# Building the table of routed rows with one-hot products instead of scattering it through memory

## The reference, cut to what matters

```
aff = sigmoid(x @ wa)                     # 16 experts per row
topk_p, topk_i = top_k(aff, 2)            # two experts per row
topk_p = topk_p / sum(topk_p)
combine = sum(one_hot(topk_i) * topk_p)   # [row, expert]
routed = einsum('bsed,bse->bsd', experts(x), combine)
shared = sum(shared_experts(x))           # two experts that every row uses
out = x1 + layernorm(x + shared + routed)
```

## Time and profile before

| what | us |
|---|---|
| median of 3 timed runs | 1720.22 |
| lowest and highest of them | 1716.72 and 1720.52 |
| span of the profiled execution | 1788.0 |
| scatters of the table issued from, to | 996.6, 1077.5 |
| readback of the table issued | 1171.3 |
| first product of the routed part | 1225.9 |

### The profile page before, as it was taken

The page is one execution under the profiler, slowest core; times in us unless marked ns, Lnnn a source line. Parts: engine busy times, 40 slices in busy tenths (PEclk is TensorE's granted clock), DMA queues, the critical chain, the costliest instruction groups (busy, mean ns, idle before and its releaser), DMA issues. The chain is left out here.

```text
span 1788.0 us, 22229 instructions
## 1 busy us (share of the span) xinstructions
PE 1513.8 (85%) x6687; PEld 950.7 (53%) x6687; DVE 835.7 (47%) x1747; ACT 767.9 (43%) x2028; POOL 535.1 (30%) x725
## 2 busy tenths in 40 slices
PE   4698989899889989986979736999999999999930
PEld 3454656565655656544768625886454444445510
DVE  4665676767668676655353401222222222222218
ACT  2677676777668687674231101111122112212205
POOL 2122322323222323222210570001433344444426
PEclk8787989899898989777999957999999999999975
DMA  5433554745554545535253502344577666565548
GB/s 162 81 58 65 106 131 96 148 90 143 98 120 113 117 101 102 131 86 205 106 187 133 95 13 82 106 92 128 127 217 188 177 146 175 143 141 123 91 60 362
DMA packets 115884, 225.61 MB, mean 126 GB/s; under 512 B 26661, under 2 KB 52854, under 8 KB 111160
## 3 DMA queue, kind: packets, MB, share of 16 engines
q1 hardware_dynamic: 96024, 182.70, 39.1%
q0 software_dynamic: 19744, 41.50, 12.4%
HBM read 219.28 MB, written 71.97 MB: 163 GB/s over the span
## 5 line engine op out<-in xcount | busy, mean ns | idle before, releaser
L2068 PE MATMUL bank<-ring,xg 128*128 x632 | 287.0, 597 | 1.0 <-issue 0.5
L1155 ACT ACTIVATE bank<-bank,mr 128x384 f32<-128x384 f32 (+3 forms) x512 | 255.5, 503 | 36.3 <-DVE mr L1380 36.3
L1380 DVE TENSOR_REDUCE mr<-bank 128x1 f32<-128x512 f32 (+3 forms) x352 | 214.8, 631 | 112.4 <-PE bank L1936 110.5
L1172 ACT ACTIVATE P<-bank 128x512 f32<-128x512 f32 x320 | 183.0, 596 | 109.2 <-PE bank L1950 107.5
L1833 POOL DMA_INDIRECT z_scratch<-wst,pl x79 | 125.0, 1582 | 281.0 <-DMA z_scratch<-wst,pl 249.8
L1934 PE MATMUL bank<-Ks,Qs 96*128 96x384 f32 (+3 forms) x512 | 173.3, 408 | 40.5 <-ACT P L1172 15.7
L1865 PE MATMUL bank<-xt,ws 128*128 128x512 f32 x768 | 186.7, 400 | 3.2 <-issue 3.2
L1690 DVE TENSOR_SCALAR wst<-bank,pl 128x512 f32<-128x512 f32 x79 | 59.3, 751 | 259.4 <-DMA z_scratch<-wst,pl 238.5
L2068 PEld LDWEIGHTS bank<-ring,xg 128*128 128x128 f32 x632 | 114.5, 191 | 118.0 <-issue 117.8
L1950 PE MATMUL bank<-Qs,Ks 98*128 98x512 f32 x320 | 154.8, 521 | 26.3 <-ACT bank L1155 12.1
L1764 POOL TENSOR_SCALAR_AFFINE_SELECT P<-P 128x256 f32<-128x256 f32 (+1 forms) x192 | 93.4, 488 | 279.3 <-ACT P L1172 276.9
(11 more groups left out here) (228 smaller groups left out, 2292.3 us busy)
## 6 DMA issues: line engine op xcount, KB each, us to landing
ring<-in_w SPq DMA_DIRECT2D x79, 1024.0 KB
ring<-in_w SPq DMA_DIRECT2D x79, 512.0 KB
Qs<-st SPq DMA_DIRECT2D x192, 128.0 KB, 4.9
xt<-xt_scratch SPq DMA_DIRECT2D x32, 512.0 KB, 6.3
xt_scratch<-xt SPq DMA_DIRECT2D x30, 512.0 KB, 5.3
z_scratch<-wst SPq DMA_DIRECT2D x33, 256.0 KB
xin<-in_x SPq DMA_DIRECT2D x8, 1024.0 KB, 6.6
rd<-rt_scratch SPq DMA_DIRECT2D x64, 128.0 KB, 2.7
```

Source lines behind the costliest of these rows:

```text
L1155: m = e.activation(ps[:, o * k:o * k + k], ps[:, o * k:o * k + k], ACT.Exp, scale=-1.0, bias=mr[:, G % 2, c:c + 1], accum_out=se[:, G % 2, ...
L1172: e.activation(Pt[:, p, :], bank[PA.bank[step]][:, :], ACT.Exp, scale=-1.0).then_inc(s_exp, 1)
L1380: e.tensor_reduce(mr[:, G % 2, 0:16].rearrange("p (h i) -> p h i", i=4)[:, h:h + n, i:i + 1], bank[PA.bank["max", b, p, j]][:, 0:n * k].re ...
L2068: e.matmul(ps[:, :].rearrange("p (o n) -> p o n", o=1), xg[:, q, 128 * k:128 * k + 128], ring[:, bass.ds(reg[n], 1), 512 * k:512 * k + 512 ...
```

## The change

The two 4-byte values of the table are now made on chip. For a place s, the lane s mod 128 and the group's first place s - s mod 128 are computed on VectorE (`lanes`, `firsts`). For each of 64 (choice, tile) pairs VectorE makes a one-hot matrix of the lane (`tA`, 128x128) and one of the group (`tB`, 128x80), and multiplies the latter by three values: the row number, the weight rounded to TensorE's format, and what the rounding left. TensorE multiplies `tA` by `tB` and adds all 64 products in one bank of 128x320. VectorE reads the bank once and makes `pw_s` (weights) and `pl` (row numbers; a place that nobody took becomes a dummy row). The 64 transfers, `nd`, `wd`, `pos`, the tensor `PL`, its filling and its readback are gone. The work is cut into 16 chunks of 4 pairs: `build` on VectorE, `fill` on TensorE two steps later, and one `read`. One accumulator bank is held from the first `fill` to `read`.

```
-    def spread():
-        for t in range(NT):
-            while ("route", 8) not in P.nth:
-                yield
-            P.add("spread", t)
+    def table():
+        while ("route", 8) not in P.nth:
             yield
+        held = None
+        for c in range(NCH + 2):
+            if c >= 2:
+                s = P.add("fill", c - 2)
+                if held is None:
+                    held = P.on(OU, s)
+                P.bank[s] = held
+            if c < NCH:
+                P.add("build", c)
+            yield
+        P.bank[P.add("read", 0)] = held
...
-    interleave((route, 1), (shared(), 1), (spread(), 2.5))
+    interleave((route, 1), (shared(), 1), (table(), 2))
...
-            w.wait_ge(nd_pool, 3)
-            e.dma_start(PL.rearrange("(n p) c -> n p c", p=128), nd[:, :, :]).then_inc(d_nd, 16)
...
-                        e.tensor_copy(pos[:, n, :], po).then_inc(route_dve, 1)
+                    e.tensor_copy(whole, both).then_inc(dve_own, chain.up())
+                    e.tensor_scalar(whole, whole, 127, None, ALU.bitwise_and).then_inc(dve_own, chain.up())
+                    e.tensor_copy(lanes[:, :, :].rearrange("p k t -> p (k t)"), whole).then_inc(dve_own, chain.up())
...
+            def build(c):
+                k, t, q = c // (NT // CH), CH * (c % (NT // CH)), c % 2
+                if c >= 2:
+                    w.wait_ge(tab_pe, c - 1)
+                e.tensor_tensor(tA[:, q, :, :], ... lane ..., ... lanes ..., ALU.is_equal).then_inc(tab_dve, 1)
+                e.tensor_tensor(tB[:, q, :, 0, :], ... steps ..., ... firsts ..., ALU.is_equal)
+                e.tensor_tensor(tB[:, q, :, 1:4, :], tB[:, q, :, 0:1, :] ..., vals[:, k, ts, :] ..., ALU.mult).then_inc(tab_dve, 1)
...
+                elif kind == "fill":
+                    w.wait_ge(tab_dve, 2 * n + 2)
+                    for i in range(CH):
+                        m = e.matmul(ps[:, 0:320], tA[:, q, i, :], tB[:, q, i, :, :] ...,
+                                     start=n == 0 and i == 0, stop=n == NCH - 1 and i == CH - 1)
+                    m.then_inc(tab_pe, 1)
...
-                    for k in range(2):
-                        e.indirect_dma_start(PL, bass.IndirectOffsetOnAxis(ap=pos[:, k, n:n + 1], axis=0), wd[:, k, n, :],
-                                             None).then_inc(d_sc, 16)
```

More of the change, by code:

```diff
@@ L24 @@
 SPLIT = ((0, 0), (0, 1), (1, 0))
+CH = 4
+NCH = 2 * NT // CH
 class Once:
@@ L504, in shared @@
             yield
-    def spread():
-        for t in range(NT):
-            while ("route", 8) not in P.nth:
-                yield
-            P.add("spread", t)
-            yield
+    def table():
+        while ("route", 8) not in P.nth:
+            yield
+        held = None
[9 more added lines that the diff above has]
+        P.bank[P.add("read", 0)] = held
+        OU.done(held)
+        OU.had[held] = ("read", 0)
     route = router()
     next(route)
-    interleave((route, 1), (shared(), 1), (spread(), 2.5))
+    interleave((route, 1), (shared(), 1), (table(), 2))
     GU, TR, OU = Banks(0, 3), Banks(3, 2), Banks(5, 3)
@@ L700, in program @@
             rb_s = sb2("rb_s", [128, 512], F32R)
+            assert here() == rest_at + 16384
             xg = sb2("xg", [128, 2, 512])
@@ L706, in program @@
             cT = sb2("cT", [80, 2, 128], F32R)
-            pos = sb2("pos", [128, 2, NT], I32)
+            vals = sb2("vals", [128, 2, NT, 3], F32R)
+            lanes = sb2("lanes", [128, 2, NT])
+            firsts = sb2("firsts", [128, 2, NT])
+            steps = sb2("steps", [128, 80])
+            dump = sb2("dump", [128, 2])
             tab = sb2("tab", [1, 3, 80], I32)
@@ L719, in program @@
             nb3 = sb2("nb3", [128, NT])
+            xg_at = rest_at + 16384
+            tA = over("tA", [128, 2, CH, 128], xg_at, F32R)
+            tB = over("tB", [128, 2, CH, 4, 80], xg_at + 4096, F32R)
+            tT = over("tT", [128, 4, 80], xg_at)
             zf = nc.alloc_sbuf_tensor_at("zf", [128, NT, 512], F32, offset=low)
@@ L768, in program @@
         moe_read_by = {"up": h_dve, "cT": cT_act, "down": zs_dve, "take": xg_act, "rup": rh_dve,
-                       "rturn": hr_act, "rdown": yo_dve}
+                       "rturn": hr_act, "rdown": yo_dve, "read": tab_read}
         def ups(n):
@@ L1650, in _ @@
                     route(n)
+                elif kind == "build":
+                    build(n)
+                elif kind == "read":
+                    w.wait_ge(tab_pe, NCH)
+                    e.tensor_copy(tT[:, :, :].rearrange("p v j -> p (v j)"), bank[PM.bank[step]][:, 0:320]).then_inc(tab_read, 1)
+                    w.wait_ge(tab_read, 1)
+                    e.tensor_tensor(pw_s[:, :], tT[:, 2, :], tT[:, 3, :], ALU.add).then_inc(pl_dve, 1)
+                    e.scalar_tensor_tensor(tT[:, 1, :], tT[:, 0, :], dump[:, 1:2], tT[:, 1, :], ALU.mult, ALU.add).then_inc(dve_own, chain.up())
+                    done()
+                    e.tensor_scalar(pl[:, :], tT[:, 1, :], dump[:, 0:1], None, ALU.add).then_inc(pl_dve, 1)
                 elif kind == "up":
@@ L1688, in _ @@
                         w.wait_ge(d_ys[o], 16 * (n // 3))
-                    w.wait_ge(d_pl[n >= 8], 16)
-                    e.tensor_scalar(yo[:, o, :], bank[PM.bank[step]][:, :], pl[:, n, 0:1].bitcast(F32), None, ALU.mult).then_inc(yo_dve, 1)
+                    w.wait_ge(pl_dve, 2)
+                    e.tensor_scalar(yo[:, o, :], bank[PM.bank[step]][:, :], pw_s[:, n:n + 1], None, ALU.mult).then_inc(yo_dve, 1)
             def last(g):
@@ L2025, in _ @@
                     e.matmul(bank[PM.bank["count"]][:, :], one_b[:, :], mb_[:, :], start=True, stop=True).then_inc(cnt_pe, 1)
+                elif kind == "fill":
+                    q, ps = n % 2, bank[PM.bank[step]]
+                    w.wait_ge(tab_dve, 2 * n + 2)
+                    if n == 0:
+                        moe_bank_free(w, step)
+                    for i in range(CH):
+                        m = e.matmul(ps[:, 0:320], tA[:, q, i, :], tB[:, q, i, :, :].rearrange("p v j -> p (v j)"),
+                                     start=n == 0 and i == 0, stop=n == NCH - 1 and i == CH - 1)
+                    m.then_inc(tab_pe, 1)
                 elif kind == "up":
```

70 lines of the change are left out of this document (44 added, 26 removed).

## The result

The changed kernel takes 1742.7 us (median of 4 runs, 1737.83 to 1747.08). The kernel before took 1720.37 us in the runs beside it (1716.72 to 1724.93). The ratio on record, an estimate over the runs of both kernels, is 1.0106, 95% interval 1.0067 to 1.0146, so it is slower; the two medians alone give 1742.7/1720.37 = 1.0130. Forecast were 1730 us and slower. The median lies 0.7 us above the range of 1714 to 1742; by the ratio it would be 1.0106 x 1720.37 = 1738.6, inside it. Beside the 9.5 us that the forecast added, 18.2 us were measured by the ratio and 22.3 by the medians.

A forecast was written before the change was run, and what follows sets the result against it. TensorE, without gaps in the shared part, was taken to bound the kernel, so added products cost their full duration. 1720.2 + 9.9 (products) + 2.6 (late `hb`) - 3 (scatters) = 1729.7, so 1730 us, range 1714 to 1742.

The forecast's parts named there:

- The stall is 65.9 us and not in the metric: TensorE's loss during the scatters in the shared part: 65.9 us, taken as a price of recording, absent from timed runs.
- Rival A: The scatters hold TensorE's signals back in every execution, recorded or not, so the change gives 1667 us; chance 0.12.
- The scatters cost 3 us in a timed run: Removing the 64 scatters gains 3 us through TensorE's late signals in the shared part, bounds 0 and 20 us.
- rival B: TensorE's signals are partly late in plain runs, 12 to 20 us, paying for the additions: 1717 us; chance 0.13.
- 64 products at 0.155 us, 9.9 us: Products of 320 columns added to TensorE's gapless shared part cost their full duration, 9.9 us, bounds 6.9 and 15.0.
- Late `hb`: 1.8 and 0.8 us, nothing in step 11, 2.6 in all: VectorE's builds delay `hb` beside route steps 9 and 10, stalling TensorE 2.6 us; bounds 0 and 16 us.
- Rival C: VectorE's queue decides each round, a build taking 3.3 us instead of 2.28: 1744 us; chance 0.07.
- Readback nothing: Removing GpSimd's wait for the table's readback gains nothing, since the first routed product waits for the last shared `wst`.
- The sum, 12.5 us of additions: The products' 9.9 us and late `hb`'s 2.6 us together, all added in the shared part.

The follow-up runs named there:

- comparisons 3 and 4: Two later sets of runs, each beside its own runs of the kernel before, which had the stall there: medians 1795.45 and 1793.64 us.
- e1_before: The kernel before, unchanged, run and profiled again: median 1726.78 us, ratio 1.0004, span 1724.5 us without the stall.
- e1_both: The changed kernel plus the old filling, 64 scatters and readback, whose data nobody uses: 1745.78 us, ratio 1.0115 to the kernel before.
- comparisons 1 and 2: The first two sets of follow-up runs, each beside its own runs of the kernel before, without the stall; its median was 1726.78 us in the first.
- e2_products: The kernel before, scatters included, plus 64 products of 320 columns on constant operands in the shared part: 1739.72 us, ratio 1.0074.
- e2_late: The changed kernel with the table's steps begun after route step 11 instead of step 8: 1736.88 us, ratio 1.0072 to the kernel before.
- e3_tail: The kernel before plus 64 products of 320 columns behind its last routed product: 1795.74 us, ratio 1.0008, stall in its trace.
- e2_builds: The kernel before, scatters included, plus only the 16 build steps on VectorE, on other operands of the same sizes: 1728.80 us, ratio 1.0029.
- e1_after: The changed kernel, unchanged, run again beside the kernel before: 1745.33 us, ratio 1.0100.
- e1_pad: The changed kernel with the small memory tensor allocated again, filled once and otherwise unused: 1740.27 us, ratio 1.0082 to the kernel before.
- e2_narrow: e2_late with products 240 columns wide instead of 320, row number stored plus one: 1734.93 us, ratio 1.0054 to the kernel before.
- e3_products: e2_products unchanged, run again where the kernel before has the stall: 1800.02 us, ratio 1.0042.
- e3_double: e2_products with 128 products instead of 64, run where the kernel before has the stall: 1807.86 us, ratio 1.0085.

## Why the forecast was right, and where it was not

The direction was right in the condition of the timed runs that it was made for, by the steps that it named, and two thirds of the measured size are explained by them. One step was wrong in its reason, and there was luck in it: beside runs of the kernel before like those of comparisons 3 and 4, the same forecast would have missed by some 65 us and on the wrong side. That 1720.22 us held no stall did follow from the span's arithmetic; that the next comparison would meet the same condition didn't.

- **The stall is 65.9 us and not in the metric.** The size is right (65.9 by e1_before). That it wasn't in the timed runs listed with the first trace is right too. The reason, "the price of recording each instruction while the scatters run", fails as it was used, to part profiled from timed runs: e1_before and e1_both are recorded and have no stall, and in comparisons 3 and 4 all 35 timed runs of the kernel before lie at 1784.64 us or above, where the highest without the stall is 1740.45. It is a condition that within one comparison was there in every run of the kernel before or in none; the first profiled execution had it, the timed runs listed with it hadn't, and the record doesn't say on which chip either ran. The span's arithmetic (1788.0 - 65.9 = 1722.1 against 1720.22) showed where 67.8 us went; it didn't show why, and I gave it a cause. The Trainium skill ("NOTIFIC — the notification-queue block", section 7.1) has the internal pipeline of the trace block hold the producer back rather than lose a record; no run here shows that pipeline. The recorded runs without a stall show that recording is not enough. That it plays a part isn't excluded: each run of the later comparisons is listed with a span, so no stall is on record in a run known to be without recording.
- **Rival A**, that the scatters hold TensorE's signals back, recorded or not, is false in comparisons 1 and 2; in 3 and 4 every run with the scatters has the stall, and there its price holds (53 us faster, measured 56). It had 0.12. The step that let it down to 0.12 was that "67.8 us would then have to come from elsewhere", which looked at one condition only.
- **The scatters cost 3 us in a timed run.** Nothing that can be told, where there is no stall. In e1_before, which has them all, 49.00 of 49 us are busy and the rounds are 8.54 to 8.59 us, and e2_products and e2_late, with and without them, differ by 0.02 us in the shared part. That TensorE's signals are late by nothing also puts rival B out: e2_products, with scatters and products, is slower, not paid by them. The Trainium skill ("DMA: Bandwidth & Descriptors", Specifications) says that transfers under 512 bytes are done as read-modify-write. No run here shows that mechanism. From 998 to 1090 us the queue of loads and stores takes 75.8% of the DMA engines' time in e1_before and 34.3% in e2_late for nearly the same data (10.5 and 10.6 MB), while the scatters' own packets take 2.9%: the 8-byte writes make other transfers late by 7 us, at no cost in the kernel's time. In the stall of e3_tail the DMA share is 0.38 and 0.11, and in that of the first trace it is 0.02 from 1040 to 1061 us, with GpSimd still issuing; so the stall isn't traffic.
- **64 products at 0.155 us, 9.9 us.** 0.148 and 9.47 (e2_products). The two rows of other widths and the column price carried this; it is 4% too high.
- **Late `hb`: 1.8 and 0.8 us, nothing in step 11, 2.6 in all.** 1.8 and 0.9; e2_late takes away 239.65 - 237.07 = 2.6. A `build` was priced at 2.28 us and has 0.68 + 0.48 + 1.16 = 2.32. Rival C, a build dearer by a microsecond, is out. A thing that I didn't price stood beside it: the clock. In e2_builds waits of 1.59 and 1.99 us were followed by 1.6 us more at the lower level.
- **Readback nothing.** The first routed product still waits for `wst` and nothing else.
- **The sum, 12.5 us of additions.** The shared part is longer by 12.0. By this alone the ratio would be 1 + 12.0/1720.4 = 1.0070, near the interval's lower end of 1.0067; measured was 1.0106.

So two things are missing in the forecast's 9.5 us: the 3 us credited to the scatters, which aren't there, and some 5 us beside the sum. The latter are seen again in comparisons 1 and 2. The kernels with products are, by their ratio's excess over 1 times 1726.6, 17.3 (e1_after), 14.2 (e1_pad), 19.9 (e1_both), 12.8 (e2_products), 12.4 (e2_late) and 9.3 us (e2_narrow) longer than before, and their shared parts 12.0, 12.0, 12.5, 9.5, 9.5 and 7.4. The excess is 5.3, 2.2, 7.4, 3.3, 2.9 and 1.9 us, each but that of e1_both within its interval, all of one sign. e2_builds, with no products, has 5.0 against 5.8. Under the stall it is 2.1 us in e3_products (7.5 against 5.4) and -0.2 in e3_double (15.3 against 15.5), so nothing shows it growing with the number of products. In the traces the first store of a shared tile, ahead of all the table's steps, comes at 931.5, 932.5 and 934.3 us in the three without added products, and at 934.0 to 945.0, mean 938.9, in the eleven with them, e3_tail included. The routed part takes 505.7 to 519.9 us in the fourteen, without such an order (514.1, 514.3 and 514.7 in the same three). The tensors' places (e1_pad) don't settle it, and e3_tail, with a queue just as much longer, reaches its first store at 937.0 and yet has a ratio of 1.0008. The executions of one kernel differ by up to 21 us among themselves (e1_before 1719.39 to 1740.45), so one trace each can't tell. The cause stays open.

Open as well is what brings the stall. The records number the chip 13 in comparison 1, without it, and 13 in comparison 3, with it, so by these numbers it isn't a property of the chip. What mattered in the scatters (their number, their pace, their form) wasn't tried under the stall, nor was a run made that is known to go unrecorded.

No version here beats the kernel before where there is no stall. Where there is one, e2_late and e2_narrow should beat the changed kernel by another 2.6 and 4.6 us; that is argued from comparison 2 and wasn't run there.

## What to carry to other kernels

When a profiled execution has a loss that the timed runs lack, don't lay it to the recording before you have set the span beside the time of that same execution, and profiled the kernel again: here a span lies 1.8 us below its own time, and a second profile had 1724.5 against 1788.0. If two conditions exist, price a change in both and say what it is worth in each; here it is 1% dearer in one and 3% cheaper in the other, because it takes away the scatters, without which no trace has the stall. On an engine without gaps, added instructions cost their issue spacing (here 64 x 0.148 us), and steps put ahead of a consumer in an in-order queue belong in the rounds where that queue carries nothing else.

## What the runs showed of the chip

- While GpSimd issues 64 indirect scatters of 128 x 8 bytes, one every 1.28 us, TensorE can fall to 1.4 us for each instruction, and what waits for its last product starts 10.4 to 56.6 us late (10.4 and 46.6 in the first trace, 18.9 and 35.3 in e3_tail, 36.7 in e3_products, 56.6 in e3_double): 66 us in all for the kernel before. Four traces here have it, and by their time all timed runs of the kernel before in two comparisons, and none in two others. VectorE's instructions keep their durations and GpSimd its pace. All of this is from recorded runs.
- The same scatters without the stall cost TensorE nothing that the traces show (237.09 us against 237.07), and let 512 KB loads land after 12.3 us instead of 5.4, and 256 KB stores after 8.7 instead of 2.1.
- Two waits of 1.59 and 1.99 us, 11 us apart, were followed by some 3 us at 0.50 of full clock, which cost 1.6 us; waits of 1.47 and 0.58 us were not.
- A product with its weight load is issued every 0.116 us at 240 columns ((235.05 - 227.62)/64), 0.148 at 320 and 0.235 at 512, which is 0.39 and 0.45 ns for each further column.
